# First layer of a four-layer model: rotation, turning and projections in one block by groups of four sequences, and all norms of the decay stage on ScalarE

## What is computed

```python
def _L0_xattn_ref(q, k, v):                    # the decay part; k = v = context
    kv = jnp.swapaxes(k * v, 0, 1)
    def step(r, kv_t):
        r = DECAY * r + kv_t
        return (r, r)
    _, rs = jax.lax.scan(step, r0, kv)
    return q * jnp.swapaxes(rs, 0, 1)

def rope(x):
    ...
    xe, xo = (x[..., 0::2], x[..., 1::2])
    return jnp.concatenate([xe * cos - xo * sin, xe * sin + xo * cos], axis=-1)

def attention(x, Wq, Wk, Wv, Wo):
    xr = rope(x)
    Q = (xr @ Wq) ...                          # 16 heads of 16
    K = (xr @ Wk) ...; V = (xr @ Wv) ...       # 4 groups of 16
    scores = jnp.einsum('bghsd,bgtd->bghst', Q, K) / jnp.sqrt(jnp.float32(D_K))
    ...

x = x + jnp.tanh(g_xattn[0]) * _L0_xattn_ref(_layernorm(x, axis=-1), ctx_1024, ctx_1024)
x = x + jnp.tanh(g_ffn[0]) * _L0_ffn_ref(_layernorm(x, axis=-1), ...)   # h = x + attention(rms_norm(x, w), ...)
```

## Time and profile before

| what | us |
|---|---|
| median of three runs | 1587.41 (1584.8 to 1591.92) |
| profiled execution | 1585.8, its span 1584.0 |
| decay stage, first statistics to the last | 5.64 to 33.77 |
| rotation stage, aggregates to the last copy to ZT | 34.81 to 60.40 |
| projection stage, first weight load to the last copy of V | 60.69 to 98.12 |
| attention, first instruction | 98.44 |

### The profile page before, as it was taken

How to read it: one execution, slowest core, us unless ns; L and a number is a source line. 1 busy time by engine, 2 the same in 40 slices (tenths; PEclk the granted TensorE clock), 3 DMA queues, 4 the chain that set the end, 5 groups by cost and what they waited for, 6 DMA issues and landing times. The chain is left out here.

```text
span 1584.0 us, 28289 instructions
## 1 busy us (share of the span) xinstructions
PE 1327.1 (84%) x9624; PEld 1112.3 (70%) x9642; DVE 1141.7 (72%) x2475; ACT 909.5 (57%) x1954; POOL 715.1 (45%) x753
## 2 busy tenths in 40 slices
PE   3689988799999999968987679999778965546898
PEld 1345566699999999844567679999766842335687
DVE  7447765689889899657967759889665658795654
ACT  3336652577777878656754248778426457464432
POOL 2223200376766766604311138888403930453444
PEclk7799996899999999989997889999989988686999
DMA  5000002566666766340013226776510000101000
GB/s 188 1 1 1 1 8 74 187 243 230 245 263 215 276 243 227 131 130 1 1 34 115 80 90 234 249 255 241 185 49 34 1 1 1 34 1 63 1 28 28
DMA packets 60828, 173.69 MB, mean 110 GB/s; under 512 B 10304, under 2 KB 42048, under 8 KB 51088
## 3 DMA queue, kind: packets, MB, share of 16 engines
q1 hardware_dynamic: 53200, 151.42, 26.8%
q0 software_dynamic: 7488, 20.46, 3.7%
HBM read 155.34 MB, written 16.52 MB: 108 GB/s over the span
## 5 line engine op out<-in xcount | busy, mean ns | idle before, releaser
L1885 POOL TENSOR_TENSOR l0m_e_DL<-l0m_e_DN,l0m_e_DH 128x256 fp32r<-128x256 f32 x192 | 174.4, 918 | 98.0 <-ACT l0m_e_DH L1728 96.5
L1793 DVE TENSOR_TENSOR l0m_e_UL<-l0m_e_U,l0m_e_UH 128x512 fp32r<-128x512 f32 x192 | 170.5, 893 | 10.9 <-ACT l0m_e_UH L1718 10.4
L1654 PE MATMUL PS<-l0m_e_CH,l0m_e_UH 128*128 128x256 f32 x480 | 138.4, 288 | 2.0 <-DVE l0m_e_CL L1828 2.0
L1654 PE MATMUL PS<-l0m_e_CH,l0m_e_UL 128*128 128x256 f32 x480 | 136.5, 284 | 0.0
L1654 PE MATMUL PS<-l0m_e_CL,l0m_e_UH 128*128 128x256 f32 x480 | 136.5, 284 | 0.0
L1718 ACT CAST l0m_e_UH<-l0m_e_U 128x512 fp32r<-128x512 f32 x192 | 117.9, 614 | 0.0
L1793 DVE TENSOR_TENSOR l1m_e_UL<-l1m_e_U,l1m_e_UH 128x512 fp32r<-128x512 f32 x96 | 85.7, 895 | 14.5 <-ACT l1m_e_UH L1718 13.6
L1654 PEld LDWEIGHTS PS<-l0m_e_CH,l0m_e_UH 128*128 128x128 f32 x480 | 92.7, 193 | 2.2 <-ACT l0m_e_UH L1718 2.2
L1687 PE MATMUL PS<-l0m_e_DH,l0m_e_HH 128*128 128x256 f32 x312 | 89.0, 285 | 4.7 <-issue 2.6
L1654 PEld LDWEIGHTS PS<-l0m_e_CH,l0m_e_UL 128*128 128x128 f32 x480 | 92.7, 193 | 0.0
L1654 PEld LDWEIGHTS PS<-l0m_e_CL,l0m_e_UH 128*128 128x128 f32 x480 | 92.7, 193 | 0.0
(11 more groups left out here) (622 smaller groups left out, 4765.7 us busy)
## 6 DMA issues: line engine op xcount, KB each, us to landing
l0m_e_U<-in_l_up SPq DMA_DIRECT2D x24, 2048.0 KB
l0m_e_DN<-in_l_down SPq DMA_DIRECT2D x24, 1024.0 KB, 5.0
l1m_e_U<-in_l_up SPq DMA_DIRECT2D x24, 1024.0 KB, 6.7
l1m_e_DN<-in_l_down SPq DMA_DIRECT2D x24, 512.0 KB, 4.0
l1a_GA<-results_by_choice SPq DMA_DIRECT2D x16, 256.0 KB, 5.8
l1m_c_GA<-results_by_choice SPq DMA_DIRECT2D x16, 256.0 KB, 4.7
Z<-in_l_b_rows SPq DMA_DIRECT2D x24, 128.0 KB, 3.2
X<-in_x SPq DMA_DIRECT2D x4, 512.0 KB, 7.4
```

The source lines that it names most:

```text
L1654: ins = nc.tensor.matmul(hb(u)[:, a * SLOTS:(a + 1) * SLOTS], w[:, f % RING, k, a, :], x[:, t % 2, k, :], start=(p == 0), stop=(p == len(p ...
L1793: nc.vector.tensor_tensor(UL[:, f % RING, :, :, :], U[:, t % 2, :, :, f * P:(f + 1) * P], UH[:, f % RING, :, :, :].bitcast(F32), ALU.subtr ...
L1885: nc.gpsimd.tensor_tensor(DL[:, f % RING, :], DN[:, t % 2, f, :], DH[:, f % RING, :].bitcast(F32), ALU.subtract).then_inc(s_dl, 1)
```

## The change

Decay stage: the norms of all sequences are ACT's (the loop at L445 runs over every sequence), DVE keeps the factors (`factors`), and DVE's order for step n becomes: variance of part n, x_stats of part n-2, factors of part n, gated products of part n-1.

First attention: the rotation and the projection block become one. The sequences go in four groups of four. DVE rotates a group at 512 columns (`rotate`), PE turns its two pairs in PSUM banks 0 and 1 (`turn`), ACT copies them to ZT (`columns`), and PE makes the group's eight jobs in a ring of the six other banks; the turn of the next group stands in PE's queue behind the second job. DVE's order is rotate 0, 1, 2, values 0, rotate 3, values 1, 2, 3. POOL's norms wait until all rotations are done.

```diff
@@ decay_layer @@
-                            for b in range(n * PB + 1, (n + 1) * PB, 2):
+                            for b in range(n * PB, (n + 1) * PB):
                                 nc.scalar.activation(Z[:, b, :], X[:, b, :], ACT.Identity, bias=SMALL[:, 2, b:b + 1],
                                                      scale=RSTD[:, b:b + 1]).then_inc(s_za, 1)
...
-                        def normalise(n):
+                        def factors(n):
...
-                            for b in range(n * PB, (n + 1) * PB, 2):
-                                nc.vector.tensor_scalar(Z[:, b, :], X[:, b, :], MV[:, b, 0:1], RSTD[:, b:b + 1],
-                                                        ALU.subtract, ALU.mult).then_inc(s_zd, 1)
...
-                            dve.wait_ge(s_zd, j + 1)
-                            dve.wait_ge(s_za, j + 1)
+                            dve.wait_ge(s_za, 2 * j + 2)
...
                             if n < PARTS:
                                 variance(n)
+                            if n >= 2:
+                                x_stats(2 * n - 4)
+                                x_stats(2 * n - 3)
+                            if n < PARTS:
+                                factors(n)
                             if n >= 1:
                                 gated(2 * n - 2)
                                 gated(2 * n - 1)
-                            if n < PARTS:
-                                normalise(n)
...
-                            if n >= 2:
-                                x_stats(2 * n - 4)
-                                x_stats(2 * n - 3)
@@ l0_attention @@
+                            GROUPS, JOBS, RING = 4, 8, 6
+                            GB = B // GROUPS
+                            bank = lambda g, j: PS[:, 2 + (g * JOBS + j) % RING, :]
...
+                                    def rotate(g):
+                                        for b in range(g * GB, (g + 1) * GB, 2):
+                                            nc.vector.tensor_scalar(ZS[:, b, :, :], apart(b), MV[:, b, 0:1],
+                                                                    RF[:, 0, b:b + 1], ALU.subtract,
+                                                                    ALU.mult).then_inc(s_zs, 1)
+                                        dve.wait_ge(s_za, (g + 1) * GB // 2)
+                                        dve.wait_ge(s_zs, (g + 1) * GB // 2)
+                                        for out, par, n in ((XR[:, group(g), 0:P], 0, 0), (TMP[:, 0, group(g), :], 1, 1),
+                                                            (XR[:, group(g), P:D], 0, 2), (TMP[:, 1, group(g), :], 1, 3)):
+                                            nc.vector.tensor_tensor(out, parity(g, par), table(n), ALU.mult).then_inc(s_p, 1)
...
+                                    for g in range(3):
+                                        rotate(g)
+                                    values(0)
+                                    rotate(3)
+                                    for g in range(1, GROUPS):
+                                        values(g)
...
+                                    for g in range(3):
+                                        normed(g)
+                                    columns(0)
+                                    normed(3)
+                                    for g in range(GROUPS):
+                                        queries_keys(g, QT, 0)
+                                        if g + 1 < GROUPS:
+                                            columns(g + 1)
+                                        queries_keys(g, KT, KD)
...
+                                    turn(0)
+                                    pe.wait_ge(s_w, 48)
+                                    for g in range(GROUPS):
+                                        pe.wait_ge(s_ta, 2 * (g + 1))
+                                        for j in range(JOBS):
+                                            emptied(pe, g, j)
...
+                                            ins.then_inc(s_full, 1)
+                                            if j == 1 and g + 1 < GROUPS:
+                                                turn(g + 1)
...
+                                def _(pool):
+                                    nc.gpsimd.memset(V[:, :, :, DH], 1.0).then_inc(s_one, 1)
+                                    pool.wait_ge(s_xr, 2 * GROUPS)
```

More of the change, by code:

```diff
@@ new lines, in values @@
+                                    def values(g):
+                                        if g == 0:
+                                            dve.wait_ge(s_one, 1)
+                                        for r in range(4):
+                                            dve.wait_ge(s_full, g * JOBS + 4 + r + 1)
+                                            rows = bank(g, 4 + r)[:, 0:NG * DH].rearrange("p (h e) -> p h e", e=DH)
+                                            nc.vector.tensor_copy(V[:, g * GB + r, :, 0:DH], rows).then_inc(s_ed, 1)
@@ L805, in _, with normed @@
                                     act.wait_ge(s_ok, 1)
-                                    for b in range(1, B, 2):
-                                        nc.scalar.activation(ZS[:, b, :, :], apart(b), ACT.Identity, bias=RF[:, 1, b:b + 1],
-                                                             scale=RF[:, 0, b:b + 1]).then_inc(s_za, 1)
-                                    for i in range(6):
-                                        act.wait_ge(s_tr, i + 1)
-                                        nc.scalar.copy(pair_target(ZT, i), pair_bank(i, F32)).then_inc(s_ta, 1)
+                                    def normed(g):
+                                        for b in range(g * GB + 1, (g + 1) * GB, 2):
+                                            nc.scalar.activation(ZS[:, b, :, :], apart(b), ACT.Identity,
+                                                                 bias=RF[:, 1, b:b + 1],
+                                                                 scale=RF[:, 0, b:b + 1]).then_inc(s_za, 1)
@@ new lines, in columns, with queries_keys @@
+                                    def columns(g):
+                                        for i in (2 * g, 2 * g + 1):
+                                            act.wait_ge(s_tr, i + 1)
+                                            nc.scalar.copy(pair_target(ZT, i), pair_bank(i % 2, F32)).then_inc(s_ta, 1)
+                                    def queries_keys(g, dst, at):
+                                        for k in range(KD):
+                                            act.wait_ge(s_full, g * JOBS + at + k + 1)
+                                            nc.scalar.copy(dst[:, k, toks(g)], bank(g, at + k)).then_inc(s_ea, 1)
@@ L826, in l0_attention, with turn @@
-                        project("l0a_qkv", W[:, :, :], [ZT], lambda n: (
-                            [cols_job(0, 0, QT, k, n) for k in range(KD)]
-                            + [cols_job(0, D, KT, k, n) for k in range(KD)]
-                            + [values_job(0, 2 * D, V, NG, n, r) for r in range(BANK // S)]), ones=V[:, :, :, DH],
-                            on_pool=normalised_rows)
+                                    def turn(g):
+                                        pe.wait_ge(s_xr, 2 * (g + 1))
+                                        for i in (2 * g, 2 * g + 1):
+                                            if g:
+                                                pe.wait_ge(s_ta, i - 1)
+                                            for k in range(KD):
+                                                for j in range(2):
+                                                    ins = nc.tensor.transpose(pair_bank(i % 2, F32)[:, k, j, :],
+                                                                              XR[:, 2 * i + j, k * P:(k + 1) * P], IDENT)
+                                            ins.then_inc(s_tr, 1)
@@ new lines, in _ @@
+                                @block.gpsimd
+                                def _(pool):
+                                    nc.gpsimd.memset(V[:, :, :, DH], 1.0).then_inc(s_one, 1)
+                                    pool.wait_ge(s_xr, 2 * GROUPS)
+                                    for b in range(B):
+                                        nc.gpsimd.tensor_scalar(Z[:, b, :], X[:, b, :], RSTD[:, b:b + 1],
+                                                                SMALL[:, 2, b:b + 1], ALU.mult, ALU.add).then_inc(s_z, 1)
+                                    pool.wait_ge(s_z, B)
```

73 lines of the change are left out of this document (35 added, 38 removed).

## The result

The kernel after takes 1573.74 us (median of eight runs, 1570.29 to 1579.38), the kernel before 1586.85 in its eight (1576.18 to 1591.92): a ratio of 0.9932, 95% interval 0.9912 to 0.9951. By that ratio it is faster by 0.7%, which is 10.8 us (7.8 to 14.0); the medians differ by 13.1 us. Forecast were 1573.9 and 13.5. The profiled execution has a span of 1571.1 for 1584.0.

The account below looks back on a forecast made before the run. DVE was taken to bound the decay and rotation stages, PE the projections. Gains of 2.9 (decay) and 10.6 us (rotation and projections) sum to 13.5: 1587.41 - 13.5 = 1573.9 us, range 1568 to 1581.

Parts of the forecast that it names:

- gain of the decay stage: Decay stage: moving DVE's norms to ACT ends the last statistics at 30.9 instead of 33.77, a gain of 2.9 us.
- first projection: Rotation by groups of four: PE begins projections at 47.05 instead of 60.69 us, 44.2 on the new clock.
- lower clock in the first group: Start of PE's projections: the half clock adds 2.35 us to the first block, possible range 0.6 to 3.0.
- a turn inside the stream: Between projections: each of three turns of eight transposes costs PE some 1.0 us, 3.0 us together.
- PE's end: End of the projections: 87.2 us on the old clock instead of 97.86, a gain of 10.6 us.
- The clock at the attention's start: First two sets of attention scores: they may run at half or full clock, some 1.5 us either way.
- The walk: Decay stage: DVE's queue timed anew step by step from row durations, last statistics at 30.9, gain 2.9 us.
- the bf16 copy: Decay stage, in the walk of DVE's queue: this copy was put at 0.2 us.
- That the decay stage gives little: Rival, decay stage: waits for POOL's additions show in full, leaving only about 1 us gain; 1575.8 us, chance 0.07.
- That the turns break the clock: Rival, projections: each of three turns returns PE to 1.2 GHz, costing another 2.35 us each; 1581 us, chance 0.05.
- That the groups do not overlap: Rival, projections: PE waits for ZT behind ACT's queue, some 1.5 us for each of three groups; 1578.4 us, chance 0.04.
- That the clock never rises: Rival, projections: with turns between them PE stays at the low clock and takes twice as long; 1608.9 us, chance 0.03.

Follow-up runs that it names:

- e5_halves: Kernel after, but VectorE rotates in two halves of eight sequences (1024 columns); the attention starts at 89.18 us for 84.67.
- e6_turn_late: Kernel after, but the next group's turn stands behind all eight jobs and its ZT copies behind the keys' copies; the attention starts at 87.52 us for 84.67.
- e4_act_only: Kernel after, but the decay stage keeps VectorE's old order, with all norms on ScalarE; the stage ends at 28.71 us for 30.98.
- e3_order_only: Kernel after, but VectorE keeps its eight decay-stage norms, in the new order; the stage ends at 32.76 us, against 33.77 in the kernel before.
- e1_decay_alone: Kernel before with only the decay stage of the kernel after; the attention starts at 95.56 us for 98.44, ratio to the kernel before 0.9982.
- e11_best: e10_warm_whole plus two matmuls of 512 columns ahead of the first attention's causal-mask wait; ratio to the kernel before 0.9882, attention starts at 79.69 us.
- e7_warm: Kernel after with five matmuls of 512 columns added ahead of PE's first turn, results overwritten; the attention starts at 83.41 us for 84.67.
- e10_warm_whole: e4_act_only with matmuls added where PE rests before and just after the first turn, results overwritten; the attention starts at 79.98 us.

## Why the prediction was right

**Point by point**, on the clock of the kernel after:

| step | forecast | measured |
|---|---|---|
| last statistics of the decay stage | 30.9 | 30.98 |
| gain of the decay stage | 2.9 | 2.8 |
| 512-wide ops, start to start | 0.60 | 0.60 |
| first projection | 44.2 | 44.39 |
| lower clock in the first group | 2.35 | 2.30 (56.22 - 44.39 - 8.65 - 0.88) |
| a turn inside the stream | 1.0 | 0.88 |
| PE's end (87.2 less the decay gain) | 84.3 | 84.09 |
| attention's start | 84.9 | 84.67 |
| time behind it | 1485.6 | 1486.4 |

Nothing of the sum is off by more than 0.4 us; the largest miss is the three turns, put at 3.0 and 2.6 as measured. PE was the bound from its first projection, as read from the earlier trace rows: the blocks are 9.53 apart (56.22 to 65.75), 8.65 and a turn. e5_halves and e6_turn_late show that it is the first piece of XR that sets its start and that the copies are hidden. The clock at the attention's start, put at up to 1.5 us either way, moved 0.4: the first reduction came 4.46 us behind POOL's first product before and 4.04 after.

**Luck.** That the median of 1573.74 lies 0.2 from the forecast is luck. The ratio is known to 6 us only, its middle is a gain of 10.8 and not 13.5, and the time behind the attention's start differed by up to 18 us between single executions (below). What bears the mechanism out is the attention's start, 13.8 us earlier for 13.5.

**Two things behind right numbers were wrong.** The first is the sentence that the code after "also moves the factors ahead of the gated products, when POOL is idle", told as part of the gain. The walk that followed had the new order's cost in its tail, and so its sum came out; but I did not walk the old order beside it. e4_act_only shows that this half of the edit loses 2.3 us; it is a gain, of 1.0, only with the norms still on DVE (e3_order_only). The second is the bf16 copy, put at 0.2 where it took 0.86 beside POOL. Other steps of the walk were too long and took most of that back: a part's variance took 1.92 and 1.94 for 2.06, x_stats 1.31 for 1.4, so that the third part's products started at 22.88 for 22.8. The forecast of DVE's rest ahead of the first V copy (6 us) was 4.64.

**The rivals.** That the decay stage gives little: no, 2.8. That the turns break the clock: no, the granted clock was 1.00 in the three turns inside the stream and after them, and in e6_turn_late with a rest besides. The Trainium skill, TensorE: Matmul & The Clock Gate, Part 4: PE-mode transpose, has it that the full clock does not engage for transposes; the traces do not agree, by these turns and by the rise at 51.8 us in the kernel before. That rise is no rule either: in e1_decay_alone the same first 16 transposes ran at 0.50 to their end (3.68 us for 3.27). That the groups do not overlap: no rest of PE in the stream. That the clock never rises: it rose 4.6 us after the first projection.

**Open:** which share of the 2.3 us of order is the bf16 copy, how the 6.4 us of the one block divide, and whether the 7.8 us more behind the attention's start in e11_best's profile are chance.

## What to carry to other kernels

Where one engine rests while another prepares its first operand, the size of the first piece goes into the end one to one: cut it small, keep the rest of the preparation beside the work (the one block was worth 6.4 us here, the small first piece 4.5), and check each queue for what waits behind what. When an edit moves work to another engine and also changes the order, walk both orders: here the move was worth 5.1 us and the order took 2.3 of them, because products that feed POOL stood behind statistics that wait for POOL. Idle time of PE ahead of a dense stretch can be filled with matmuls whose results nobody reads: filled up to the first projection but for 0.4 us it won 2.7 us here, and with the last two rests left open 1.3.

## What the runs showed of the hardware that I had not expected

In e7_warm the granted clock fell at 44.2, when dense matmuls had begun again, after a rest of 1.8 us, a turn of 1.09 and a rest of 0.8; in e6_turn_late it stayed at 1.00 through three rests of 0.73 with 10 us of dense work between them.

The rise does not come at a fixed distance from the start of the work. In e10_warm_whole it came at 36.9, 5.7 us after the first added matmul, and in e11_best, with the same code up to there, at 34.7, 3.1 us after it. In e11_best the added matmuls were done before XR was, and the first turn was not held up: it started at 39.78 for 40.13, though the decay stage had ended 0.4 later.

The time from the attention's start to the end, the same code in eleven of the twelve kernels, was 1478.6 us in e1_decay_alone and 1496.6 in e6_turn_late, and anything between in the others (1485.6 before, 1486.4 after, 1492.1 in e4_act_only, 1496.2 in e3_order_only). A part of it lies between the first write of the tile l0m_XN and that of l0m_e_HL, where the first experts' tokens are gathered: 64.1 us in e1_decay_alone, 69.1 after. With one execution of each, a difference of a few microseconds in the whole says nothing, while the ends of the stages ahead of it agree much better: the decay stage of the kernel after ends between 30.89 and 31.11 in the five kernels that have it, e4_act_only's between 28.71 and 29.14 in three.
